# Computing the low part of the keys on POOL instead of VectorE, with the order of the calls laid out anew

## The reference

```python
xn = layernorm(x)
# attention: 32 query heads, 8 key/value heads, 128 wide, rotary positions, causal
q, k, v = rotary(xn @ Wq.T), rotary(xn @ Wk.T), xn @ Wv.T
attn = softmax(causal(q @ k.T / sqrt(128))) @ v        # four query heads share a key head
# experts: 16 experts of width 128, two chosen per token, and one shared expert of width 256
h = silu(xn @ w1 + b1) * (xn @ w2 + b2)
moe = sum(gate[e] * (h_e @ w3[e] + b3[e])) + shared(xn)
out = x + attn @ Wo.T + moe
```

## Time and profile before

| | us |
|---|---|
| median of 3 runs | 911.94 (909.39 to 912.68) |
| the profiled execution | 912.02 |
| its span, first to last instruction | 910.3 |
| PE busy | 870.0 (96% of the span) |
| DVE busy | 705.4 (77%) |
| POOL busy | 515.9 (57%) |
| ACT busy | 432.0 (47%) |
| mean granted TensorE clock | 0.992 |

### The profile page before, as it was taken

One profiled execution on the slowest core, in us unless ns is written; L12 is line 12 of the kernel. 1 busy time (PEld: TensorE's weight loads), 2 busy tenths in 40 slices (PEclk: granted clock), 3 DMA queues, 4 the chain that ended last, 5 costly groups with the idle time before them and its releaser, 6 DMA issues.

```text
span 910.3 us, 16509 instructions
## 1 busy us (share of the span) xinstructions
PE 870.0 (96%) x4638; PEld 728.9 (80%) x4638; DVE 705.4 (77%) x1551; ACT 432.0 (47%) x1074; POOL 515.9 (57%) x614
## 2 busy tenths in 40 slices
PE   8999999999899989999899998999899998999987
PEld 7788778888688878888788877888788877888775
DVE  5656778778868797788867798778877798688885
ACT  3512353365454554545444554455445554455442
POOL 5835656445655556655555466555455466554572
PEclk9999999999999999999999999999999999999999
DMA  9935571113422353242522353232623253231252
GB/s 336 325 116 185 184 249 59 47 53 113 154 76 99 94 188 98 90 141 77 187 76 98 86 179 95 101 120 74 202 87 105 86 173 92 84 117 43 87 163 75
DMA packets 71249, 114.11 MB, mean 125 GB/s; under 512 B 6448, under 2 KB 34736, under 8 KB 70960
## 3 DMA queue, kind: packets, MB, share of 16 engines
q1 hardware_dynamic: 68656, 105.32, 36.2%
q0 software_dynamic: 2560, 8.39, 2.8%
HBM read 82.76 MB, written 30.93 MB: 125 GB/s over the span
## 4 chain that ended last, share of the span: by engine, by line
PE 69%; DVE 11%; issue 8%; DMA 7%; POOL 3%; ACT 1%; SPq 1%; DVEq 0%; ACTq 0%; POOLq 0%
PE bank L1994 7%; PE bank L1996 6%; PE bank L1995 6%; DMA w_raw<-w 6%; PE bank L2242 5%; PE bank L2246 5%; PE bank L2243 5%; PE bank L2129 5%; PE bank L2131 5%; PE bank L2130 5%; PE bank L2208 4%; PE bank L2223 3%; PE bank L2226 3%; PE bank L2224 3%; PE bank L2150 1%
## 5 line engine op out<-in xcount | busy, mean ns | idle before, releaser
L658 POOL TENSOR_SCALAR prob<-prob,rsum 128x128 f32<-128x128 f32 (+3 forms) x256 | 145.3, 587 | 187.5 <-DVE rsum L1492 187.4
L890 ACT ACTIVATE prob<-bank,nmax 128x128 f32<-128x128 f32 (+3 forms) x256 | 133.0, 526 | 129.9 <-DVE nmax L1486 127.7
L1486 DVE CUSTOM_DVE_ANT_0 bank<-bank,causal 128x128 f32<-128x128 f32 (+3 forms) x256 | 122.4, 501 | 54.5 <-PE bank L1996 51.7
L1514 DVE TENSOR_TENSOR pT_lo<-bank,pT_hi 128x512 fp32r<-128x512 f32 x160 | 108.1, 683 | 37.4 <-ACT pT_hi L913 36.3
L913 ACT ACTIVATE pT_hi<-bank 128x512 fp32r<-128x512 f32 x160 | 92.8, 595 | 67.2 <-PE bank L2208 37.1
L2242 PE MATMUL bank<-wo_lo,oT_hi 128*128 128x512 f32 x256 | 103.2, 403 | 0.8 <-DVE wo_lo L1532 0.8
L2129 PE MATMUL bank<-xT_hi,wq_lo 128*128 128x512 f32 x256 | 102.3, 400 | 0.6 <-DVE rot L1446 0.6
L2131 PE MATMUL bank<-xT_hi,wq_hi 128*128 128x512 f32 x256 | 102.0, 399 | 0.0
L2130 PE MATMUL bank<-xT_lo,wq_hi 128*128 128x512 f32 x256 | 101.3, 396 | 0.0
L2246 PE MATMUL bank<-wo_hi,oT_lo 128*128 128x512 f32 x256 | 100.9, 394 | 0.0
L2243 PE MATMUL bank<-wo_hi,oT_hi 128*128 128x512 f32 x256 | 100.7, 393 | 0.0
(11 more groups left out here) (225 smaller groups left out, 2215.8 us busy)
## 6 DMA issues: line engine op xcount, KB each, us to landing
w_raw<-w SPq DMA_DIRECT2D x31, 512.0 KB, 3.9
wq_raw<-wq SPq DMA_DIRECT2D x32, 256.0 KB, 6.0
v_all<-v_stage SPq DMA_DIRECT2D x16, 512.0 KB
v<-v_all SPq DMA_DIRECT2D x16, 512.0 KB, 6.1
wo_raw<-wo SPq DMA_DIRECT2D x32, 256.0 KB, 3.2
xg<-x_slots SPq DMA_DIRECT2D x31, 256.0 KB, 3.7
eb<-b SPq DMA_DIRECT2D x31, 256.0 KB, 3.8
w_raw<-w SPq DMA_DIRECT2D x31, 256.0 KB, 2.8
```

What stands on the lines that cost most here:

```text
L658: last = nc.gpsimd.tensor_scalar(row, row, rsum[:, stat(b, i, h)], 1.0, ALU.mult, ALU.mult)
L890: last = nc.scalar.activation(prob[n % 2][:, h, 0:P * (i + 1)], bank[S_BANKS[use % 2]][:, 256 * k:256 * k + P * (i + 1)], ACT.Exp, bias=nm ...
L1486: last = nc.vector.tensor_tensor_reduce(s, s, causal[:, TB * P - width:TB * P], -1.0, -MASKED * 3.0, ALU.add, ALU.min, nmax[:, stat(b, i, h)])
```

## The change

`lo_kT` moves from DVE's lists into POOL's, as the same subtraction; there are 16 of them, two a pass. Because `krot` is now read by POOL last, `turn_k` on DVE gets a wait for the `lo_kT` before it. And all the lists of all engines are written in another order, with the same calls in them otherwise. The lists are too long to show; the diff shows the new function, the wait, POOL's list for a pass of the loop, and the calls of PE, ACT, DVE and SP that are named below.

```diff
@@ POOL
+            def lo_kT(g, b):
+                if no_head(g):
+                    return
+                pool.wait_ge(kT_hi_ok, count(1, g, b, 1))
+                nc.gpsimd.tensor_tensor(kT_lo[:, b, :], krot[:, 0, :], kT_hi[:, b, :].bitcast(F32),
+                                        ALU.subtract).then_inc(kT_split, 1)
...
@@ POOL, key_head
                 normalise(g, 0, 0)
                 normalise(g, 0, 1)
+                add_q(g, 1, 0)
                 add_k(g, 1)
                 lo_w12(tile_of(g, 1))
                 split_k(g + 1)
-                add_q(g, 1, 0)
                 normalise(g, 0, 2)
+                lo_w3(tile_of(g, 1))
+                lo_kT(g, 1)
                 add_q(g, 1, 1)
-                lo_w3(tile_of(g, 1))
                 add_q(g, 1, 2)
                 lo_w12(tile_of(g, 2))
+                split_q(g + 1, 0)
                 normalise(g, 0, 3)
...
                 normalise(g, 1, 2)
                 lo_w12(tile_of(g, 4))
-                add_k(g + 1, 0)
+                lo_kT(g + 1, 0)
                 add_q(g + 1, 0, 1)
...
@@ DVE, turn_k
                 dve.wait_ge(k_psum, count(1, g, b, 1))
+                wait_count(dve, kT_split, count(1, g, b, 0))
...
@@ DVE
-            def lo_kT(g, b):
-                if no_head(g):
-                    return
-                dve.wait_ge(kT_hi_ok, count(1, g, b, 1))
-                nc.vector.tensor_tensor(kT_lo[:, b, :], krot[:, 0, :], kT_hi[:, b, :].bitcast(F32),
-                                        ALU.subtract).then_inc(kT_split, 1)
...
@@ SP, key_head
+                load_w3(tile_of(g, 2), e2)
                 load_wq(g, 3)
```

More of the change, by code:

```diff
@@ L786, in last_head @@
                 add_q(g, 1, 0)
+                lo_kT(g, 1)
+                normalise(g, 0, 2)
                 add_q(g, 1, 1)
-                lo_w3(tile_of(g, 0))
-                normalise(g, 0, 2)
+                normalise(g, 0, 3)
                 add_q(g, 1, 2)
-                normalise(g, 0, 3)
                 add_q(g, 1, 3)
@@ L1673, in first_head @@
-                maxima(g, 0, 3, 1)
-                lo_pT(g, 0, 1, 0)
-                lo_wo(g, 0)
-                lo_oT(g, 0, 0)
                 maxima(g, 0, 3, 2)
                 maxima(g, 0, 3, 3)
-                lo_pT(g, 0, 1, 1)
+                lo_wo(g, 0)
+                lo_wo(g, 1)
+                lo_oT(g, 0, 0)
                 lo_q(g, 1, 1)
-                lo_wo(g, 1)
+                lo_wo(g, 2)
+                lo_wo(g, 3)
+                turn_q1(g, 1, 2)
+                turn_q2(g, 1, 2)
@@ L1786, in key_head @@
                 expert_product(tile_of(g, 1))
-                lo_pT(g, 0, 1, 1)
+                maxima(g, 0, 3, 3)
+                lo_q(g, 1, 1)
+                expert_hidden(tile_of(g, 1))
+                lo_wo(g, 0)
                 lo_wo(g, 1)
                 lo_wo(g, 2)
+                lo_hT(tile_of(g, 1))
                 lo_wo(g, 3)
-                expert_hidden(tile_of(g, 1))
-                lo_q(g, 1, 1)
                 turn_q1(g, 1, 2)
                 turn_q2(g, 1, 2)
-                maxima(g, 0, 3, 2)
+                add_b3(tile_of(g, 1))
@@ L1796, in key_head @@
                 lo_pT(g, 0, 2, 0)
-                lo_hT(tile_of(g, 1))
-                lo_kT(g, 1)
-                maxima(g, 0, 3, 3)
+                lo_pT(g, 0, 2, 1)
+                lo_oT(g, 0, 1)
                 add_out(g, 0, 0)
-                add_b3(tile_of(g, 1))
-                lo_oT(g, 0, 1)
+                lo_xg(tile_of(g, 2))
                 lo_q(g, 1, 2)
                 inverse_sums(g, 0, 3)
-                lo_xg(tile_of(g, 2))
+                maxima(g, 1, 0, 0)
                 turn_q1(g, 1, 3)
-                lo_pT(g, 0, 2, 1)
+                turn_q2(g, 1, 3)
@@ L1914, in last_head @@
+                add_out(g - 1, 1, 3)
+                lo_q(g, 1, 1)
                 maxima(g, 0, 3, 2)
-                lo_q(g, 1, 1)
                 maxima(g, 0, 3, 3)
-                add_out(g - 1, 1, 3)
+                lo_pT(g, 0, 2, 0)
                 lo_oT(g, 0, 1)
-                lo_pT(g, 0, 2, 0)
-                lo_pT(g, 0, 2, 1)
-                lo_hT(tile_of(g, 0))
-                turn_q1(g, 1, 2)
-                turn_q2(g, 1, 2)
-                lo_wo(g, 0)
-                lo_wo(g, 1)
@@ L1926, in last_head @@
-                inverse_sums(g, 0, 3)
+                turn_q1(g, 1, 2)
+                inverse_sums(g, 0, 3)
+                turn_q2(g, 1, 2)
+                lo_hT(tile_of(g, 0))
+                lo_wo(g, 1)
+                lo_pT(g, 0, 2, 1)
                 maxima(g, 1, 3, 0)
+                maxima(g, 1, 3, 1)
+                add_b3(tile_of(g, 0))
+                lo_wo(g, 2)
                 lo_q(g, 1, 2)
-                add_b3(tile_of(g, 0))
+                lo_wo(g, 3)
+                lo_pT(g, 0, 2, 2)
@@ L2477, in key_head @@
                 scores(g, 0, 1, 0)
+                project_k(g, 1, 3)
+                values(g - 1, 1, 3, 2)
+                expert_up(tile_of(g, 0))
                 scores(g, 0, 1, 1)
-                project_out(g - 1, 1, 2, 0)
-                project_out(g - 1, 1, 2, 1)
-                values(g - 1, 1, 3, 2)
-                project_out(g - 1, 1, 2, 2)
-                transpose_h(tile_of(g, 0))
-                transpose_p(g, 0, 0, 0)
-                scores(g, 0, 2, 0)
                 values(g - 1, 1, 3, 3)
@@ L2627, in last_head @@
                 project_k(g, 1, 2)
-                project_k(g, 1, 3)
-                scores(g, 0, 0, 1)
                 values(g - 1, 1, 3, 0)
```

1003 lines of the change are left out of this document (501 added, 502 removed).

## The result

The changed kernel takes 875.15 us (median of 4 runs, 873.52 to 876.43); the kernel before took 910.66 (4 runs, 907.15 to 912.68). The ratio is 0.961, 95% interval 0.958 to 0.965: faster by 3.9%, by 35.5 us. The forecast was 896, its low end 884. The direction held and the size did not: the gain is more than twice the forecast one.

The account below looks back on a forecast made before the run. PE's waits and clock were taken to bound the kernel. From the profiled execution, 912.0 - 14.3 - 10.6 - 4.9 + 14 = 896.2, said as 896; low end 884, high end 913, the forecast's own range 888 to 900.

Parts of the forecast that it names:

- What bounds the kernel: Only PE's idle time and clock can be won: 25.7 us of waits plus 4.1 of clock, 29.8 in all.
- `lo_kT` off DVE, -14.3: In the loop, `transpose_x`'s 10.2 us wait behind `add_b3` goes, and with it 4.1 us of clock.
- `lo_kT` on POOL, 0: 16 subtractions of 1.30 us each on POOL, which is busy 57%; nothing on the path.
- The order, -10.6 and -4.9: Reordered lists remove PE's waits for `hi_hT`'s tile (8.0) and `exps` (2.6), and `transpose_h`'s wait (4.9).
- What the order puts in, +14: New waits at tight places in the loop, 2.3 us a pass; bounds +2 and +36.
- the five places: `project_q(g, 1, 0)`, tile 0's `expert_down`, row block 2's `scores`, `project_q(g, 1, 3)`, tile 2's `w3`: 0.4 to 3.5 us together.
- The clock, 4.1 of the -14.3: Three loop passes run slow at 0.98, mean 104.43 against 103.07 us; this goes with the second idle stretch.
- First and last pass, 0: New order at both ends costs nothing: first pass between -3 and +3, last between -3 and +2.
- The rule: DVE and POOL share an SBUF port, so moving work from one to the other might not help.
- The rivals: The lock moves along (chance 0.13), the new order is tighter than the old (0.12), only `lo_kT` pays (0.2).
- The lock: POOL's `lo_kT` stops another DVE instruction where PE waits, 15.6 us back: 912, within 0.5%; chance 0.13.
- Only `lo_kT` pays: The waits behind DMAs return at other calls: 898 and up to 905; chance 0.2.

Follow-up runs that it names:

- e1: Kernel before, old order kept, with only `lo_kT` moved from DVE to POOL: 897.53 us, ratio 0.988.
- e4: Kernel before with the loop's `lo_kT(g, 1)` still on DVE but three calls later, behind `add_b3` of tile 1: 895.74 us, ratio 0.985.
- e9: Kernel before with only POOL's `lo_w12` of tile 2 in the loop moved behind `normalise(g, 0, 3)`: 927.33 us, ratio 1.019.
- e3: Kernel before with one swap in ACT's loop list, `hi_hT` of tile 1 ahead of `hi_w12` of tile 2: 891.04 us, ratio 0.979.
- e2: Changed kernel's new order, but with `lo_kT` kept on DVE: 874.81 us, ratio 0.963.
- e5: Kernel before with four loop calls moved on ACT, DVE and POOL, no operation on another engine: 882.1 us, ratio 0.970.
- e12: e2 with only POOL's `normalise` of row block 1 moved ahead of the last four gathers at the end: 877.28 us, ratio 0.965.
- e7: e2 with DVE's loop `lo_kT` moved behind `lo_oT(g, 0, 1)`, where POOL's w12 piece of tile 2 runs: 898.2 us, ratio 0.987.

## Why the prediction was wrong in size and right in kind

**What bounds the kernel**: right. PE's waits and its clock were the only thing to win. The changed kernel's loop passes have 98.47 us of PE work in 98.55.

**`lo_kT` off DVE, -14.3**: right. e1 gave 12.8, e4 14.5; e9 shows that POOL's piece beside it was the cause. What I did not see is that the late `hi_hT` had brought the two together (e3). The wait was one link of a chain, and four different edits each remove it (e1, e3, e4, e9).

**`lo_kT` on POOL, 0**: right, 1.30 us each, and no reader waits. With the new order the move itself is worth 0 (e2, 0.3 us apart). For the time, the change is its order.

**The order, -10.6 and -4.9**: right; the waits for `hT_lo`, `exps` and `h_rows` are gone. Together with the first term that is 29.8 us, and the loop gained 32.0. e5 leaves SP's list as it was and comes within 0.55 us a pass of the new order, so little can hang on the moved loads.

**What the order puts in, +14**: this step failed. It measured 0.24 us a pass, 1.4 in all, below the lowest bound I gave it (6 x 0.4 = 2). Of the five places, tile 0 was sized right (0.1 to 0.3 short, measured 0.24). `project_k` to `project_q(g, 1, 0)` has 0.6 to spare (`turn_k` ends at 395.93, its reader starts at 396.54; I said 0.3). `project_q(g, 1, 3)` has 0.26 to spare where I said 0 to 0.5 short. The `exps` of row block 2 and the `w3` of tile 2 cause no wait. My own sum of the places allowed 0.4 (as listed they add to 0.4 to 2.6; the 3.5 has a collision on top that did not come). I put 2.3 because the order before has 4.3 us of waits a pass. That borrowed the old order's average for the new one. It had no row behind it: e3 shows that 14.6 of those 25.7 us hang on one late call (10.2 for `eb` and 4.4 of `hT_lo`), so the 4.3 is not a rate at which such an order waits. e5, which has two such new places, pays 1.1 in the pass read. With 1.4 for this term the sum would have been 883.6; of the 19.8 us between 896.2 and the 876.4 measured it is 12.6.

**The clock, 4.1 of the -14.3**: right that it comes back, all passes of the loop are at 1.00. The reading under it was not. By the mark of the first `scores` the passes before take 104.7, 103.0, 104.1, 104.1, 104.1 and 103.2 us, and the slow clock is in the first, third and fifth. So the fourth is long at full clock (its wait for `hT_lo` is 1.81 us), and the 104.5 and 103.2 of the prediction come from a mark that was off. The fourth and the fifth:

```profile
502.30:606.39 104.09, 98.72 (x545) 83.83 (x544) 82.53 (x183) 52.60 (x134) 59.47 (x70) 1.00 0.37 115
606.39:710.50 104.11, 100.36 (x545) 85.17 (x544) 82.60 (x183) 52.60 (x134) 59.41 (x70) 0.98 0.36 115
```

The price of the low clock is in PE's busy time: 100.4 a pass against 98.75, so 1.66, or 5.0 in three passes. In the time of the passes it is 0.9 each, 2.7 in all, because PE idles less in the slower passes (3.9 against 4.7 us). The 4.1 lies between. That it comes back because the `eb` wait goes is not shown: e1 has no such wait in its profile, and three of its four executions are at 0.994 to 0.996. All four of the changed kernel are at 0.998; in its profile the clock falls only in the last pass, behind its waits (0.72 from 855 to 861) and at the very end (0.95 from 867 on).

**First and last pass, 0**: measured -3.7 (2.0 ahead of the loop, 1.7 behind it), within the bounds, of which the -2.0 ahead of the loop is within what equal code shows (e12).

**Sum with the measured terms**: 912.0 - 14.3 - 10.6 - 4.9 + 1.4 - 3.7 = 879.9. The profiled execution after took 876.4, so 3.5 us are in none of my terms. They are in the loop: it gained 32.0, while 29.8 - 1.4 = 28.4 are accounted for. PE's own time there tells where most of it is: its idle time fell from 25.7 to 0.5 us and its busy time from 597.5 to 590.8. Of that 6.7, 5.0 is the low clock, and 1.7 is what a pass at full clock had more (98.75 against 98.47). The sum has 4.1 for both, 2.6 too little. The 1.7 fits the restart behind each wait, which no wait names: the matmul at 439.18 in the earlier trace rows is followed by the next at 439.48, after 0.30 us and not 0.23. About 1 us of idle time stays unexplained.

**The rule**: I set the Trainium skill (Perfetto Trace Analysis, Optimizing Scalar/DVE Operations) against the change; it says that moving work between the two engines might not help, for they share a port. Taken by itself it is borne out in the new order: e2 and the changed kernel are 0.3 us apart. In the order before, the move gained 12.8 us (e1), yet e4 gained as much without it.

**The rivals**: none came for this change. The lock did not move to another reader that PE waits for: `expert_hidden` of tile 2 still takes 0.99 us, hidden. "Only `lo_kT` pays" would fit e1, where the order stays as it was.

## What to carry to other kernels

Where several engines work off fixed lists, follow a slow instruction back to what put it there before pricing it: one late copy on ACT stood behind two of the waits, and moving that one call gave more than half of the whole gain. Price a new order by the margin of each reader, from the rows of that place; here the share of waits in the old order was no measure of the new one. And when an instruction is moved, look up its own reader first: e7 and e9 missed because a reader stood nearer than the one I watched.

## What the hardware showed

**A collision by instruction, not by load.** In e7, beside the same instruction of POOL (434.18 to 436.56), DVE's subtraction with one input in a PSUM bank took its usual 0.68 us, and the next one, with both inputs in SBUF, stood still and ended 0.55 us behind POOL's. It is the 0.54 of the earlier trace rows. In these rows the one that started first kept its usual time: in e3 DVE started 0.34 earlier, kept its 0.68, and POOL's piece took 2.62 instead of 2.39. The Trainium skill (SBUF — State Buffer, Who interferes with whom) states this: the port pair that the two engines share is locked exclusively, a DVE instruction with two SBUF inputs contends with one of GpSimd that reads SBUF, and the order of issue decides who waits. The traces here agree, in both directions.

**The clock behind a wait.** A wait of 2.1 us in e7 and one of 4.3 in e9 are each followed by about 4 us at a granted clock near 0.55. In e9:

```profile
454.50:458.50 4.00, 3.94 (x16) 3.69 (x17) 0.00 (x0) 0.00 (x0) 3.16 (x4) 0.57 0.06 9
```

So in e7 the wait cost nearly twice its length (3.82 us a pass for a wait of 2.08). The length of a wait alone does not decide it. In e1 and e4 PE waited for `hT_lo` up to 1.89 and 1.98 us at a time, and e1 has a longer wait than e7's in its last pass:

```profile
866.93 0.50 PE L2227 MATMUL bank<-pT_lo,v 128*128 128x512 f32 x1 [2.38 <-DVE pT_lo L1521]
```

The mean clock of both profiled executions is 1.000: behind none of these did it fall. In the kernel before it fell in the passes with waits of 1.12 to 1.17 and 1.69 to 1.75 us (first, third, fifth) and not in those with 1.81 and 1.70 or 1.73 and 1.70 (fourth and sixth). And other executions of the same e1 kernel have 0.994 to 0.996. The runs don't show what tells the cases apart.
